# The shared expert of a mixture-of-experts layer, with weights and tokens exchanging places on TensorE

## The chip, the cores and the metric

The kernel runs on one core of one Trainium2 chip. The metric is the device time of one execution in microseconds (us). TensorE multiplies, VectorE (DVE), ScalarE (ACT) and GpSimd (POOL) work beside it, SyncE (SP) issues DMAs.

## The reference

2048 tokens of width 512 pass a pre-norm block: a linear attention with decay (16 heads), then a mixture of experts (8 experts of 352 hidden columns, the best two of each token) and one shared expert of 704 hidden columns, which all tokens pass.

```python
x = x + attn(layernorm(x))           # decayed running sums of k*v and k
x2 = layernorm(x)
g = silu(einsum('td,edh->teh', x2, w_gate)) * einsum('td,edh->teh', x2, w_up)
routed = einsum('teh,ehd,te->td', g, w_down, comb)
shared = silu(x2 @ sw_gate) * (x2 @ sw_up) @ sw_down
x = x + routed + shared
```

## The kernel before

Every factor is kept as two halves, an upper float16 and the lower rest, and every product is three products (upper x upper, upper x lower, lower x upper): `product`, line 591. The kernel writes out each engine's order by hand, with semaphores between engines; nothing plans it.

**Attention** takes four blocks of 512 tokens. Beside its last block the shared expert begins (lines 778 to 803), and its normalised rows go to a scratch in HBM, from where a transposing DMA brings tiles of 128 tokens back (`turn_tile`, line 900) into one of two buffers `xT[:, b]`.

**The shared expert** is 32 units: unit u is half u % 2 of the hidden columns (384, then 320) for the tile u // 2 of 128 tokens. A tile of x is the stationary operand, the weights stream past it. The result lies with tokens on the partitions, so the hidden values must be turned before the down product: `turn_chunk` (line 639) puts three 128x128 transposes between the next unit's gate products. A unit is, on TensorE (lines 805 to 831): gate(u+1) with turns of u, up(u+1), the beside work, down(u). Half 1 has a twin: the last 64 hidden columns stand in two copies, so that its last chunk needs two products and not three; 17 down products a tile. ScalarE (`gate_silu`, `upper_hidT`, lines 1274 to 1282) applies silu and copies the upper half; VectorE (`hidden`, `rest_hidT`, lines 1554 to 1578) multiplies and makes the lower half. Each pair of buffers passes a semaphore: `g_mm`, `u_mm`, `silu_s`, `hid_s`, `turned_h`, `hidTh_s`, `hidT_s`, `y_mm`, `y_s`.

**Beside the units** the 24 weight matrices of the eight experts are prepared, one piece per unit from unit 3 to 26: ScalarE squares it (`square`, line 1226, waits for the norm of the piece before), VectorE folds the squares (`fold`, 1588), TensorE sums columns (`column_norms`, 444, waits for the fold), VectorE takes the maximum (`column_max`, 1598), and one unit in three sets scales (`set_scales`, 1605). Units 8 to 30 split the pieces (`split_unit`, line 321; `upper` on ScalarE, 1245; `split` on VectorE, 1628), unit 19 two of them. ScalarE also issues the loads of experts 2 to 7 in units 5, 8, 11, 14, 17 and 20 (line 1371). VectorE chooses experts and builds the tables of jobs (`routing`, line 1968), with one-hots in the even units 10 to 24 (`one_hots`, 1914) that TensorE multiplies (`table_product`, 706). In iteration u each engine first does the unit's own steps, then this work in this order: VectorE one-hots, maximum, scales, split, fold, routing; ScalarE load, upper, square, y. On TensorE the norms of unit u come in iteration u + 1.

**The jobs** (line 833) are 36 groups of 128 rows of one expert, four of them pairs of 64 rows of two experts on two column tiles (`pair_product`, 601), with gathers and scatters by GpSimd (`gather`, `scatter`). A job is gate of the next, with the turns inside, up of the next, down of this one.

## Time and profile before

| | us |
|---|---|
| median of 3 runs | 656.45 (653.41 to 658.42) |
| profiled execution, its own time | 656.56 |
| its span in the trace | 654.8 |

| engine | busy us | share of the span |
|---|---|---|
| TensorE products (PE) | 625.2 | 95% |
| TensorE weight loads (PEld) | 416.1 | 64% |
| VectorE | 420.0 | 64% |
| ScalarE | 265.1 | 40% |
| GpSimd | 191.2 | 29% |

The stages, by TensorE's timeline: attention to 212.8 us, the seam in which attention ends and the shared expert begins to about 251, units of the shared expert to 422.0, jobs to about 645, last scatter and end to 654.8. The mean granted clock of TensorE was 0.988. Durations of TensorE's rows include its pipeline; what a product costs when they follow each other is the distance from start to start.

### The profile page before, as it was taken

What the parts mean: (1) busy time and instruction counts of PE and PEld (TensorE: products, weight loads), DVE (VectorE), ACT (ScalarE), POOL (GpSimd) and SP (SyncE); (2) the same over time, 40 slices, a digit from 0 to 9 for tenths busy, and PEclk for the clock granted to TensorE, in tenths of its full rate; (3) what the DMA queues carried; (4) which work ended last, traced back from release to release, by engine and by line L of the source; (5) the groups of instructions that cost most, each with busy time, mean ns of one, the idle gap of its engine ahead of it and who ended that gap; (6) DMA issues with size and microseconds to landing.
All of it is one profiled execution on the core that took longest, in us unless ns stands there. A gap on an engine that the chain in (4) does not pass through costs nothing.

```text
span 654.8 us, 11594 instructions
## 1 busy us (share of the span) xinstructions
PE 625.2 (95%) x3785; PEld 416.1 (64%) x3786; DVE 420.0 (64%) x831; ACT 265.1 (40%) x411; POOL 191.2 (29%) x250
## 2 busy tenths in 40 slices
PE   7999999999999999999999999999999999999992
PEld 7777777668677666556665556665666666555561
DVE  5998887997998954768867877633334334333331
ACT  4464653464444445466666766421111111111110
POOL 5220131231103226002111212134454354343422
PEclk8999999999999999999999999999999999998997
DMA  6851013513424796966664824469598679877743
GB/s 223 288 181 33 17 50 79 162 49 98 130 65 106 219 234 221 213 160 178 133 175 112 193 38 62 85 129 122 105 140 146 117 132 133 125 101 126 127 65 47
DMA packets 107136, 83.78 MB, mean 128 GB/s; under 512 B 77040, under 2 KB 83184, under 8 KB 107088
## 3 DMA queue, kind: packets, MB, share of 16 engines
q1 hardware_dynamic: 85744, 43.28, 29.4%
q0 software_dynamic: 12128, 26.88, 23.5%
q10 hardware_dynamic: 9216, 12.98, 6.2%
q8 instruction: 29, 0.48, 0.3%
q14 instruction: 19, 0.16, 0.1%
HBM read 43.80 MB, written 22.54 MB: 101 GB/s over the span
## 4 chain that ended last, share of the span: by engine, by line
PE 62%; DVE 5%; DMA 4%; issue 2%; SPq 1%; ACT 1%; ACTq 0%; POOL 0%; POOLq 0%; DVEq 0%
PE ps_y L597 16%; PE ps_g L597 15%; PE ps_u L597 14%; PE ring L441 8%; PE turn_h L647 3%; DMA out_dram<-y_job,job_tok 1%; PE ps_g L610 1%; DMA x_in<-x_job 1%; PE ps_u L610 1%; PE ps_y L610 1%; PE ps_y L664 1%; DMA out_dram<-x 1%; SPq L896 1%; DMA xg_odd<-xn_hl 1%; DMA x_job<-xn_scratch,job_tok 1%
## 5 line engine op out<-in xcount | busy, mean ns | idle before, releaser
L1282 ACT CAST hidT<-turn_h 128x384 f16<-128x384 f32 x68 | 32.5, 478 | 181.5 <-PE turn_h L647 181.5
L441 PE MATMUL ring<-xnT_h,wq_h 128*128 128x512 f32 x188 | 76.7, 408 | 2.7 <-DVE wq_l L1439 1.4
L597 PE MATMUL ps_g<-routed,x_in 128*128 x384 | 74.3, 316 | 2.4 <-DMA x_in<-x_job 2.4
L441 PE MATMUL ring<-xnT_h,wq_l 128*128 128x512 f32 x188 | 74.5, 396 | 0.0
L441 PE MATMUL ring<-xnT_l,wq_h 128*128 128x512 f32 x188 | 74.0, 394 | 0.0
L597 PE MATMUL ps_g<-shared,x_in 128*128 128x384 f16 (+1 forms) x384 | 72.3, 313 | 0.0
L1130 POOL DMA_INDIRECT out_dram<-y_job,job_tok x32 | 52.1, 1629 | 60.0 <-DVE y_job L1965 32.8
L597 PE MATMUL ps_y<-routed,hidT 128*128 x288 | 67.4, 379 | 1.3 <-DVE hidT L1562 1.3
L1577 DVE SCALAR_TENSOR_TENSOR hid<-ps_u,job_hid,silu 128x352 f32<-128x352 f32 x36 | 21.0, 584 | 66.9 <-PE ps_u L597 41.8
L597 PE MATMUL ps_u<-routed,x_in 128*128 x384 | 63.0, 314 | 0.0
L597 PE MATMUL ps_u<-shared,x_in 128*128 128x384 f16 (+1 forms) x384 | 62.5, 313 | 0.0
L1029 POOL TENSOR_SCALAR var_eps<-mean_var 128x1 f32<-128x1 f32 x32 | 11.5, 361 | 170.4 <-DVE mean_var L1542 92.7
L597 PE MATMUL ps_y<-shared,hidT 128*128 128x512 f16 x240 | 57.1, 379 | 3.9 <-DVE hidT L1562 2.3
L1965 DVE TENSOR_SCALAR y_job<-ps_y,job_y 128x512 f32<-128x512 f32 x36 | 27.0, 751 | 48.5 <-PE ps_y L597 43.1
L1107 POOL DMA_DIRECT2D out_dram<-y_job x16 | 14.2, 909 | 136.6 <-ACT y_job L1288 136.3
L647 PE MATMUL turn_h<-ident,hid 128*128 128x128 f32 x204 | 52.3, 274 | 0.0
L597 PEld LDWEIGHTS ps_g<-routed,x_in 128*128 128x128 f16 x384 | 37.6, 99 | 22.4 <-issue 5.0
L597 PEld LDWEIGHTS ps_u<-routed,x_in 128*128 128x128 f16 x384 | 37.8, 99 | 20.2
L597 PEld LDWEIGHTS ps_u<-shared,x_in 128*128 128x128 f16 x384 | 37.5, 98 | 19.8 <-DVE hid L1577 0.2
L597 PEld LDWEIGHTS ps_g<-shared,x_in 128*128 128x128 f16 x384 | 37.3, 98 | 20.0 <-issue 1.6
L1117 POOL DMA_INDIRECT x_job<-xn_scratch,job_tok x36 | 36.7, 1021 | 42.5 <-DMA x_in<-x_job 29.0
L597 PEld LDWEIGHTS ps_y<-routed,hidT 128*128 128x128 f16 x288 | 27.9, 98 | 31.7 <-issue 2.6
(301 smaller groups left out, 1191.1 us busy)
## 6 DMA issues: line engine op xcount, KB each, us to landing
x_res<-in_L_attn_x_dram SPq DMA_DIRECT2D x20, 256.0 KB, 3.2
routed<-in_L_ffn_w_gate_dram ACTq DMA_DIRECT2D x6, 704.0 KB, 4.8
routed<-in_L_ffn_w_up_dram ACTq DMA_DIRECT2D x6, 704.0 KB, 7.2
out_dram<-x SPq DMA_DIRECT2D x16, 256.0 KB, 3.5
xn_scratch<-xn_hl SPq DMA_DIRECT2D x16, 256.0 KB, 2.6
out_dram<-y_job POOLq DMA_DIRECT2D x16, 256.0 KB, 4.1
x_in<-in_L_attn_x_dram SPq DMA_DIRECT2D x12, 256.0 KB, 3.0
routed<-in_L_ffn_w_down_dram ACTq DMA_DIRECT2D x6, 512.0 KB, 8.2
```

The lines of the kernel that those rows point to most:

```text
L441: ins = pe.matmul(ps, a, b, start=(i == 0), stop=(i == len(steps) - 1))
L597: ins = pe.matmul(ps, a[i][:, k, :], w(j, k), start=(start and q == 0), stop=(stop and q == len(steps) - 1))
L610: ins = pe.matmul(ps[rows, :], a[i][:, k, rows], ws[h](j, k), start=(q == 0), stop=(q == len(steps) - 1), tile_position=(0, HALF * h))
L647: ins = pe.transpose(turn_h[:, c, :], hid[:, col:col + P], ident[:, :])
L664: ins = pe.matmul(ps_y[:, :], hidT[:, 0, FC - 1, :], w(j, FC - 1), start=False, stop=(stop and j == 1))
L1029: pool.tensor_scalar(ve, mv, LN_EPS, by, ALU.add, ALU.mult).then_inc(s[got], 1)
L1107: pool.dma_start(out[t * P:(t + 1) * P, :], y_job[:, t % 2, :], accum_op=ALU.add)\
L1117: pool.indirect_dma_start(x_job[:, b, :], None, xn2_d[:, :], bass.IndirectOffsetOnAxis(job_tok[:, r:r + 1], 0))\
L1130: pool.indirect_dma_start(out[:, :], bass.IndirectOffsetOnAxis(job_tok[:, r:r + 1], 0), y_job[:, b, :], None, bounds_check=T - 1, oob_is_e ...
L1282: act.copy(hidT[:, 0], turn_h[:, 0:FC, :]).then_inc(s["hidTh_s"], 1)
L1577: dve.scalar_tensor_tensor(out=hid[:, 0:n], in0=ps_u[:, 0:n], scalar=by, in1=silu[:, 0:n], op0=ALU.mult, op1=ALU.mult).then_inc(s["hid_s"], 1)
L1965: dve.tensor_scalar(y_job[:, b, :], ps_y[:, :], job_y[:, bass.ds(r, 1)], None, ALU.mult)\
```

## The change

The shared expert's weights become the stationary operand and two tiles of x (256 tokens) stream past them. The result lies with hidden columns on the partitions and needs no turn. 704 hidden columns are five whole steps of 128 and a rest of 64; the rest uses two column tiles for gate and up (one per tile of tokens) and two row tiles for down, so that a tile has 16.5 down products' time if both run at once. Six steps of a pair of tiles fill three iterations of u, the fourth holds the down products of both tiles, with the work beside them at chunk 3 of the second tile. gate and up alternate between two PSUM banks each (gate from the second pair of tiles on), the y results too. VectorE multiplies in place in PSUM. Silu, hidden values and y share SBUF in one buffer `work`, in which shared y has one slot. Both x tiles are fetched for the next pair when all up products of this pair are done. The first job's gate and up products now follow the last down product, and the jobs' turns stand in a row in front of the fourth gate product.

```diff
@@ constants
-    SHARED_F = (P * FC, HALVES * F - P * FC)
-    TWIN = P // 2
+    WHOLE = HALVES * F // P
+    REST = HALVES * F - P * WHOLE
+    STEPS = WHOLE + 1
+    SHARED_STEPS = STEPS * SBLOCKS
@@ banks
+        def gate_bank(h):
+            return ps_g if h < STEPS or h % STEPS % 2 == 0 else ps_gate
+        def up_bank(h):
+            return ps_u if h % STEPS % 2 == 0 else ps_u2
@@ product: the turns
-                    if inside is not None and 3 <= q < 3 + FC:
-                        inside(q - 3)
+                    if q == 3 and inside is not None:
+                        inside()
@@ TensorE, new
+            def shared_product(ps, h, kind):
+                ...
+                    if c < WHOLE:
+                        ins = pe.matmul(ps[:, 0:SBLK].rearrange("p (b q) -> p b q", b=2), w, xT[:, :, i * KC + k, :],
+                                        start=first, stop=last)
+                    else:
+                        for b in range(2):
+                            ins = pe.matmul(ps[REST * b:REST * (b + 1), 0:P], w, xT[:, b, i * KC + k, :],
+                                            start=first, stop=last, tile_position=(0, REST * b))
+            def shared_gate(h):
+                n, c = divmod(h, STEPS)
+                if c == 0:
+                    for b in range(2):
+                        pe.wait_ge(s[f"xin{b}"], 16 * (n + 1))
+                if 0 < h <= STEPS:
+                    pe.wait_ge(s["silu_s"], h)
+                elif h > STEPS:
+                    pe.wait_ge(s["silu_s"], h - 1)
+                if h == STEPS + 1:
+                    pe.wait_ge(s["rt_exp_in"], 1)
+                shared_product(gate_bank(h), h, 0).then_inc(s["g_mm"], 1)
+            def shared_up(h):
+                if h >= 2:
+                    pe.wait_ge(s["hidT_s"], h - 1)
+                shared_product(up_bank(h), h, 1).then_inc(s["u_mm"], 1)
+            def shared_down(n, between=None):
+                for b in range(2):
+                    ...
+                    for c in range(WHOLE):
+                        if b == 1 and c == FC and between is not None:
+                            between()
+                        pe.wait_ge(s["hidT_s"], STEPS * n + c + 1)
+                        for i, j in PARTS_OF:
+                            pe.matmul(y_bank(t)[:, :], hid_whole[:, c, i, b * P:(b + 1) * P], w(j, c), ...)
+                pe.wait_ge(s["hidT_s"], STEPS * (n + 1))
+                for i, j in PARTS_OF:
+                    for b in range(2):
+                        rows = slice(REST * b, REST * (b + 1))
+                        ins = pe.matmul(y_bank(b)[:, :], hid_rest[rows, i, :], w(j, WHOLE, rows), ...,
+                                        tile_position=(REST * b, 0))
@@ TensorE, the units
+            for u in range(2, HALVES * NT):
+                n, p = u // 4, u % 4
+                def beside():
+                    if u == 3:
+                        gate(last + 2)
+                        gate(last + 3)
+                    if norm_unit(u - 1) is not None:
+                        column_norms(norm_unit(u - 1))
+                    ...
+                if p == 3:
+                    shared_down(n, beside)
+                    continue
+                for h in (STEPS * n + 2 * p, STEPS * n + 2 * p + 1):
+                    shared_gate(h)
+                    shared_up(h)
+                    if u == 2:
+                        gate(last + h - 2 * p)
+                beside()
@@ SyncE
-                    sp.wait_ge(s["u_mm"], HALVES * (t - 1))
+                    sp.wait_ge(s["u_mm"], STEPS * (t // 2))
@@ ScalarE
+            def shared_silu(h):
+                act.wait_ge(s["g_mm"], h + 1)
+                if h:
+                    act.wait_ge(s["hid_s"], h)
+                act.activation(silu_sh[:, 0:n], gate_bank(h)[:, 0:n], ACT.Silu, ...)
+            def shared_upper(h):
+                act.wait_ge(s["hid_s"], h + 1)
+                act.copy(hidden_to(h, 0), up_bank(h)[:, 0:step_cols(h)]).then_inc(s["hidTh_s"], 1)
@@ ScalarE, the end of the seam: order
+            shared_upper(1)
+            rows_2(last + 1)
+            rows_2(last + 2)
+            shared_upper(2)
+            shared_silu(3)
+            rows_2(last + 3)
+            shared_upper(3)
@@ ScalarE, a unit: silu and upper of its two steps, then as before; y
+                if p == 3:
+                    move_y(2 * n)
+                if p == 0:
+                    move_y(2 * n - 1)
@@ VectorE
+            def shared_hidden(h):
+                dve.wait_ge(s["silu_s"], h + 1)
+                dve.wait_ge(s["u_mm"], h + 1)
+                dve.scalar_tensor_tensor(out=up, in0=up, scalar=hid_scale[:, E:E + 1], in1=silu_sh[:, 0:n], ...)
+            def shared_rest(h):
+                dve.wait_ge(s["hidTh_s"], h + 1)
+                dve.tensor_tensor(hidden_to(h, 1), up_bank(h)[:, 0:step_cols(h)], hidden_to(h, 0), ALU.subtract)
+            for u in range(2, HALVES * NT):
+                if p < 3:
+                    for h in (STEPS * n + 2 * p, STEPS * n + 2 * p + 1):
+                        shared_hidden(h)
+                        shared_rest(h)
@@ VectorE, first job
+                if first:
+                    dve.wait_ge(*tile_sem("yo", NT - 1))
```

## Rows read from the trace of the kernel before

**Rows 1.** Busy time by stretch, the rewritten stage; columns named in the first line.

```profile
core 0: us, PE busy (x) PEld busy (x) DVE busy (x) ACT busy (x) POOL busy (x), PEclk, DMA share, GB/s
...
251.20:422.00 170.80, 167.26 (x1063) 104.43 (x1062) 126.87 (x372) 108.52 (x137) 33.19 (x57) 1.00 0.61 140
```

**Rows 2.** Timeline of TensorE: start us, length us, engine, line, out<-in, count.

```profile
261.05 2.10 PE L597 MATMUL ps_y<-shared,hidT 128*128 128x512 f16 x9
262.99 0.65 PE L597 MATMUL ps_g<-shared,x_in 128*128 128x384 f16 x3
263.48 0.27 PE L647 MATMUL turn_h<-ident,hid 128*128 128x128 f32 x1
263.59 0.33 PE L597 MATMUL ps_g<-shared,x_in 128*128 128x384 f16 x1
```

**Rows 3.** Timeline of TensorE at the start, and the products of line 716 by duration.

```profile
13.94 1.50 PE L716 MATMUL ring<-ones_h 128*128 128x128 bf16 x24
...
L716 PE MATMUL ring<-ones_h x120: 219/219/314, 1.1 to 15.2; 128*128 128x128 bf16 x120
```

**Rows 4.** Timeline of TensorE in the first gate product of a pair job.

```profile
451.35 0.31 PE L610 MATMUL ps_g<-routed,x_in 128*64 x1
451.35 0.31 PE L610 MATMUL ps_g<-shared,x_in 128*64 128x352 f16 x1
451.50 0.31 PE L610 MATMUL ps_g<-routed,x_in 128*64 x1
...
451.75 0.55 PE L647 MATMUL turn_h<-ident,hid 128*128 128x128 f32 x3
452.22 0.34 PE L610 MATMUL ps_g<-routed,x_in 128*64 x1
```

**Rows 5.** Groups of VectorE, 262 to 420 us: busy us, mean ns, idle before.

```profile
L1633 DVE SCALAR_TENSOR_TENSOR routed<-routed,scale 128x1408 f16<-128x1408 f32 x16 | 26.9, 1678 | 5.0 <-ACT routed L1254 4.9
...
L1558 DVE TENSOR_TENSOR hidT<-turn_h,hidT 128x256 f16<-128x256 f32 x13 | 5.5, 421 | 0.9 <-ACT hidT L1282 0.7
```

**Rows 6.** The same view of ScalarE.

```profile
L1254 ACT ACTIVATE routed<-routed,scale 128x1408 f16<-128x1408 f32 x16 | 23.4, 1464 | 10.8 <-DVE routed L1633 6.8 <-issue 4.0
...
L1240 ACT ACTIVATE squares<-routed 128x1408 bf16<-128x1408 f32 x8 | 11.0, 1373 | 2.4 <-PE ps_norm L457 2.4
```

**Rows 7.** Timeline of VectorE in unit 10.

```profile
299.18 0.68 DVE L1921 TENSOR_TENSOR hot_p<-iota_p,slot_p 128x512 f16<-128x512 f32 x1
...
302.65 1.82 DVE L1633 SCALAR_TENSOR_TENSOR routed<-routed,scale 128x1536 f16<-128x1536 f32 x1
...
304.45 0.42 DVE L1558 TENSOR_TENSOR hidT<-turn_h,hidT 128x256 f16<-128x256 f32 x1
```

**Rows 8.** Timeline of VectorE in unit 5, the first slots.

```profile
269.82 0.28 DVE L1832 COPY score<-ps_rt 128x128 f32<-128x128 f32 x1
...
273.57 0.17 DVE L1855 TENSOR_TENSOR left_by<-left_by,whole_end 128x8 f32<-128x8 f32 x1
```

**Rows 9.** Timeline of ScalarE and its DMA queue (ACTq) in unit 8.

```profile
284.75 0.38 ACTq L423 DMA_DIRECT2D routed<-in_L_ffn_w_gate_dram  x1
...
287.25 1.47 ACT L1254 ACTIVATE routed<-routed,scale 128x1408 f16<-128x1408 f32 x1 [1.97 <-issue]
```

**Rows 10.** Timeline of ScalarE, the last attention tile.

```profile
242.57 0.62 ACT L1224 CAST xn_hl<-xn 128x512 f16<-128x512 f32 x1
```

**Rows 11.** DMA issues (KB, median us to landing), and the issue time of line 906.

```profile
out_dram<-y_job POOLq DMA_DIRECT2D x16, 256.0 KB, 4.1
...
xg_odd<-xn_hl SPq DMA_TRANSPOSE x8, 3.1
...
L906 SPq DMA_TRANSPOSE x_in<-xn_scratch x16: 1232/1281/1593, 184.3 to 397.2; - x16
```

**Rows 12.** TensorE behind a wait in the jobs, and the granted clock then.

```profile
590.34 0.62 PE L597 MATMUL ps_g<-routed,x_in 128*128 x3 [2.37 <-DMA x_in<-x_job]
...
592.00:594.00 2.00, 2.00 (x9) 1.01 (x8) 0.56 (x1) 0.33 (x2) 1.58 (x1) 0.50 0.51 143
```

More of the change, by code:

```diff
@@ L605, in pair_product @@
                     if q == 3 and inside is not None:
-                        for c in range(FC):
-                            inside(c)
+                        inside()
                     for h in range(2):
@@ new lines, in down_product @@
+            def down_product(u, t, w):
+                pe.wait_ge(s["hidT_s"], u + 1)
+                pe.wait_ge(s["y_s"], t)
+                product(ps_y[:, :], [hidT[:, h] for h in range(2)], w, FC, True, True).then_inc(s["y_mm"], 1)
+            halfword = lambda w, j, n, at, m: w[:, j * n + at:j * n + at + m]
+            PARTS_OF = ((0, 0), (0, 1), (1, 0))
+            def shared_product(ps, h, kind):
+                c = h % STEPS
+                steps = [(i, j, k) for k in chunks for i, j in PARTS_OF]
+                for q, (i, j, k) in enumerate(steps):
+                    w = halfword(shared_done[HALVES * kind + k // 2], j, GU, (k % 2) * HALVES * F + c * P,
+                                 P if c < WHOLE else REST)
+                    first, last = q == 0, q == len(steps) - 1
+                    if c < WHOLE:
[5 more added lines that the diff above has]
+                                            start=first, stop=last, tile_position=(0, REST * b))
+                return ins
@@ L992, in _ @@
                             turn_rows((n - 1) * TPB + j)
[L993 to L995 removed]
+            for t in range(2, NT):
                 turn_tile(t)
@@ L1577, in hidden @@
-                dve.scalar_tensor_tensor(out=hid[:, 0:n], in0=ps_u[:, 0:n], scalar=by, in1=silu[:, 0:n],
+                if r is not None:
+                    dve.wait_ge(s["turned_h"], r)
+                dve.scalar_tensor_tensor(out=hid[:, :], in0=ps_u[:, 0:F], scalar=by, in1=silu[:, :],
                                          op0=ALU.mult, op1=ALU.mult).then_inc(s["hid_s"], 1)
```

314 lines of the change are left out of this document (141 added, 173 removed).

## Prediction

> **What bounds the kernel now.** I read the span by stages first [rows 1]: from 251.2 us, where the third tile's first gate product starts, to 422.0 us, where the first job's does, lies the stage that the change rewrites. TensorE is busy for 167.3 of its 170.8 us at clock 1.00, so it is the bound and loses only 3.5 us to waits. VectorE is busy for 126.9 us there (74%) and ScalarE for 108.5 us (64%): they are hidden, but not idle, and how much room they keep is the question. Then I read TensorE's timeline for what one product costs. Nine products of 512 columns start at 261.05 and the next group at 262.99 [rows 2]: 215.6 ns each, start to start (the duration of one row holds the pipeline and isn't its cost). Products of 128 columns with 128x128 weights: 24 rows span 1.50 us, the last is 219 ns long, so (1.50 - 0.22)/23 = 55.6 ns [rows 3]. The line through both is n/2.4 + 2.3 ns: 109 ns for 256 columns, 162 for 384, 136 for 320. A turn between gate products adds 0.11 us (263.48 to 263.59) [rows 2].
>
> **What TensorE saves.** Before, for two tiles: gate and up are 48 products of 384 columns and 48 of 320, 14.3 us; 34 down products 7.33; 12 turns 1.32; together 23.0 us. After, for two tiles: five whole steps of 24 products of 256 columns, 120 x 109 ns = 13.1 us; the rest step; 30 down products, 6.47; the rest's down, six products in three couples of row tiles, between 3 x 216 ns = 0.65 (parallel) and 1.29 (one after another). The rest step has 24 couples of 128-column products on two column tiles. No row has this couple. Below, it costs one 128-column product, 55.6 ns [rows 3]; above, what a couple of 352 columns takes, 150 ns (451.35 to 451.50) [rows 4]. Those rows show both column tiles running at once, so I lean to the lower end but not onto it, since two weight loads must fit beside 53 ns of columns: 85 ns, 2.04 us. A change of tiling shows a gap, 0.10 us before the turns (451.50 + 0.15 to 451.75) and 0.14 behind them (0.47 less 3 x 0.11) [rows 4]: about 0.4 us for the four changes of a pair of tiles. With the rest's down at 0.65 (column tiles do run at once) this is 22.7 us: 0.3 us less than before, not the 1.3 us of the turns. The saved turns and the half product are nearly spent on short products.
>
> The Trainium skill, "TensorEngine Tiling (Array Packing)", Restrictions, says that column tiling disables Fast Weight Load, and "TensorE: Matmul & The Clock Gate", LDWEIGHTS, gives columns/1.2 ns for a plain load: 53 ns for 64 columns, 107 ns for a couple, so by these pages the rest step would be 24 x 0.107 = 2.6 us and the saving gone (an estimate). No row shows it: at 352 columns the load hides.
>
> **What takes the turns' place.** Step h now goes silu (ScalarE), product in place (VectorE), upper half (ScalarE), lower half (VectorE); up(h) waits for the lower half of h-2, gate(h) for silu(h-2). So TensorE may be two steps ahead, 5.2 us. Before, one unit's look-ahead was 6 us, and, more important, ScalarE was done with unit u+1's silu before its own other work, whereas now its last copy of a unit comes 1.2 us after TensorE's last product of that unit. The other work (call it the load of a unit) is unchanged: splitting an expert's piece costs ScalarE 1.4 us and then VectorE 1.6 [rows 5, 6], a square 1.3 [rows 6], the one-hots, a maximum and the scales 3.5 us of VectorE (299.18 to 302.65) and with the split and fold 5.3 us (to 304.45) [rows 7], the first slots 4.0 us [rows 8]. An expert's load holds ScalarE for 2.5 us (284.75 to 287.25) [rows 9]. And TensorE's column norms of unit u wait for the fold of u-1, which stands behind all this; they stand right behind the second step of a unit, or inside the down products at chunk 3 of the second tile.
>
> **One pair in full, units 16 to 19**, in us from its first gate product; small operations of 256 columns 0.35 to 0.4 [rows 5], handing over 0.1 to 0.3. Steps 0 and 1 end at 5.24, their lower halves at 6.85. Unit 16 on VectorE: one-hots to 8.3, maximum and scales to 10.35, split to 12.1, fold 12.2. TensorE ends step 3 and the last norms at 11.0 and waits to 12.2. Steps 2 and 3 get their halves by 14.95; step 4 and the rest end at 17.1. ScalarE issues the expert's load 14.5 to 17.0, upper half to 18.4; VectorE splits to 20.05, fold 20.15: TensorE waits 3.0. The down products run from 20.4, the norms in them come at 25.55, but unit 18 (halves 23.2, one-hots, scales, split, fold of gate weights) ends at 28.45: 2.9 more. The pair ends at 31.1, where TensorE's own work is 22.7, and 23.6 with the norms (352 columns), the tables (108) and the gaps beside them. The same working gives 29.2 for units 4 to 7 (the fold of unit 5 waits for a square behind a load, the first slots come behind it, and down chunk 4 waits for its half), 30.9 for 8 to 11, 27.2 for 12 to 15, 28.2 for 20 to 23, 25.6 for 24 to 27 and 23.7 for 28 to 31, where no load is left. Sum 195.9 against 170.8 before: **+25.1 us**.
>
> **The seams.** In front, silu(4) now stands behind the last tile's cast, which ends at 243.2 [rows 10]; then lower half and product of step 3, 245.3; rest step 247.3; gates and down products 7.9: pair 2 starts at 255.2, before it was 251.2: +4.0. At 422.0 the kernel of before still owed a down product and turns, 1.7 + 0.3: -2.0. At the end the two y copies share one buffer: copy, issue, landing 4.1 us [rows 11], twice, hold the first job's weighing on VectorE to about 11.5 us behind the last down product, 2 us after it could run; about +1 on TensorE. The next pair's two transposes are issued at the start of the down products: 1.3 each to issue and 3.1 from issue to landing [rows 11], 1.3 + 3.1 to 2.6 + 3.1 = 5.7, under 7.3 of down: nothing. The jobs' turns in a row cost nothing: in a row they are also 0.11 apart (0.47 with the gap) [rows 4], the gap there belongs to the change of tiling; the work hidden beside them is the same. If each of the 31 plain jobs showed the 0.14 gap it would be +4, if turning earlier helped, 0. Gates, gathers and scatters of the jobs stay as they are.
>
> **Sum.** The profiled execution took 656.6 us (span 654.8), 0.1 above the median of 656.45: 656.6 + 25.1 + 4.0 - 2.0 + 1.0 = **684.7 us**.
>
> **Rivals.** *Slower, as worked out*: 684.7. If half the waits are overrated, (195.9 - 165.2)/2 = 15 us less, 670; if row tiles run one after another and couples take 150 ns, up to 2.2 us a pair more where waits don't cover it, and each of the five waits over 2.2 us may halve the clock: after 2.37 us idle it is granted at 0.50, and 9 products start in 2.0 us where 2.0/0.149 = 13 would [rows 12]: 1 to 2 us each, 7 us in all, partly given back as VectorE gains that time. So 668 to 697.
> *Even*: VectorE and ScalarE keep up as they do now. 7 x 23.6 + 3.5 us of waits = 168.7, -2.1; with the seams +3.0: 657.5. For it: today's order hides 5.3 us of load, whose next lower half (304.45) came nearly in time [rows 7]. Against: in the pair above the room from the lower half to the moment that TensorE asks for the fold is 6.85 to 11.0, 4.1 us, in the first unit, and 14.95 to 17.1, 2.2 us, in the second.
> *Faster*: TensorE stays the bound and never waits (-2.1 - 3.5), both column tiles run wholly at once (24 x 0.03 x 8 = -5.8) and the front isn't late (-1.0): 644. It decides if the fold of a unit with split and scales ends less than 4 us (first unit) or 2 us (second) behind the lower half of its last step; below that every turn saved counts. VectorE's 74% speaks for it, the order of its work against.
> *Transposes late*: under an expert's load the second lands over 7.3 us after issue, on every pair 1 to 2 us, on top of the first case: about 700.
>
> **Numbers.** Slower as worked out 0.66, transposes late too 0.05, even 0.17, faster 0.12. The time is that of the first, 684. The range 652 to 697 takes in the even case and leaves out the faster one and the late transposes (0.17); the first case's own is 668 to 697. About 1% is what can be told from no change: faster 0.12, within 0.17, slower 0.71.
>
> **What would show it.** The stage up to the first job's gate should last about 199 us with TensorE idle for some 25 to 30 us, waiting for row sums or squares (the fold) and for the lower halves; the norms inside the down products should wait longest, in the units that split and set scales. In a stretch without experts (the last four units) a pair should take 23.7 us; over 24.5 means the rest step or the row tiles cost more than said. If the whole stage shows under 8 us of idle time, the step that fails is that the fold binds. If the plain jobs take longer than now, it is the turns in a row.

## The result, and the profile after

The changed kernel takes 688.22 us (median of 4 runs, 684.33 to 692.28) against 656.6 us for the kernel before on the same chip: ratio 1.0488, interval 1.0444 to 1.0532. It is 4.9% slower. The profiled execution took 686.96 us, with a span of 685.2. The forecast was 684, with 652 to 697.

First the stage that was rewritten, by pairs of tiles (busy time by stretch; the columns are those of [rows 1]). The first line is the whole stage, from the second pair's first gate product to the first job's, and answers to the line of [rows 1]:

```profile
256.70:451.80 195.10, 167.07 (x1496) 116.48 (x1496) 128.67 (x374) 107.02 (x162) 29.65 (x53) 0.97 0.49 121
256.70:287.40 30.70, 25.55 (x214) 17.34 (x214) 19.24 (x110) 12.49 (x22) 8.02 (x23) 0.94 0.63 170
287.40:319.00 31.60, 24.89 (x213) 16.39 (x211) 21.57 (x61) 17.05 (x25) 1.73 (x2) 0.95 0.62 171
319.00:345.50 26.50, 23.06 (x219) 16.68 (x217) 16.53 (x41) 16.38 (x24) 3.93 (x6) 1.00 0.49 127
345.50:376.60 31.10, 24.77 (x220) 16.95 (x218) 20.47 (x49) 16.74 (x25) 3.94 (x6) 0.96 0.44 110
376.60:404.00 27.40, 23.72 (x220) 16.64 (x218) 18.16 (x40) 18.34 (x27) 3.95 (x6) 0.99 0.50 123
404.00:429.10 25.10, 22.93 (x218) 16.57 (x217) 17.11 (x48) 16.09 (x25) 3.94 (x6) 1.00 0.28 48
429.10:451.80 22.70, 22.15 (x206) 15.91 (x204) 15.60 (x29) 9.93 (x17) 4.14 (x4) 1.00 0.37 71
```

TensorE is busy for 167.1 us, as before (167.3), and the stage is 24.3 us longer: TensorE stands still for 28.0 us where it stood for 3.5. VectorE and ScalarE have the same work as before (128.7 and 107.0 us busy; 126.9 and 108.5).

That TensorE's busy time is equal hides two things that cancel. The granted clock (third column from the end) is 0.94, 0.95, 0.96 and 0.99 in four of the pairs and was 1.00 before [rows 1]. The first of them alone lost (1 - 0.94) x 30.7 = 1.8 us, and the four 1.8 + 1.6 + 1.2 + 0.3 = 4.9 us. So the work itself is about 162 us, 5 less than before: the change did save TensorE work, and gave it back at the lower clock. Twelve down products behind a wait:

```profile
280.68 4.38 PE L737 MATMUL ps_y<-shared,work 128*128 128x512 f16 x12 [2.31 <-DVE work L1649]
```

They take 4.17 us to the next start (284.85), where twelve at the full clock take 2.59 (12 x 215.6 ns). The sum of the idle time by what ended it (waits in the window 250 to 450: engine, line, releaser, us in total, times, longest):

```profile
PE turn_h L483 <- DVE row_sum_h L1677: 15.3, 9, 3.4
PE turn_h L488 <- DVE squares L1679: 7.4, 4, 2.3
PE ps_y L737 <- DVE work L1649: 3.0, 3, 2.3
```

Lines 483 and 488 are the column norms, released by VectorE's fold: 22.7 us in 13 waits, 7.3 of them in three waits inside the down products (the longest, 3.40, among them) and 15.4 behind a unit's second step. Line 1649 is a lower half. The pair that the prediction worked out in full, units 16 to 19, starts at 345.55 (timeline of TensorE, its waits; VectorE and ScalarE around the second of them; the last bracket is the idle time and its releaser):

```profile
357.74 0.18 PE L483 MATMUL turn_h<-row_sum_h,ones_h 128*128 128x1 bf16 x1 [1.15 <-DVE row_sum_h L1677]
365.20 0.18 PE L483 MATMUL turn_h<-row_sum_h,ones_h 128*128 128x1 bf16 x1 [3.08 <-DVE row_sum_h L1677]
372.78 0.47 PE L488 MATMUL turn_h<-squares,ones_h 128*128 128x352 bf16 x2 [2.11 <-DVE squares L1679]
```

```profile
359.43 0.37 ACTq L454 DMA_DIRECT2D routed<-in_L_ffn_w_gate_dram  x1
...
360.40 1.39 ACTq L454 DMA_DIRECT2D routed<-in_L_ffn_w_down_dram  x2
361.89 1.47 ACT L1326 ACTIVATE routed<-routed,scale 128x1408 f16<-128x1408 f32 x1 [2.09 <-issue]
...
363.39 1.69 DVE L1717 SCALAR_TENSOR_TENSOR routed<-routed,scale 128x1408 f16<-128x1408 f32 x1 [3.07 <-ACT routed L1326]
364.99 0.15 DVE L1677 CAST row_sum_h<-row_sum 128x1 bf16<-128x1 f32 x1
```

This is the chain of one wait: ScalarE issues an expert's load for 2.4 us, then writes the upper half; VectorE idles 3.07 us for it, splits for 1.69, and only then comes to a cast of one column, for which TensorE has waited 3.08 us.

The seams (timeline of TensorE; the second fence is the first stretch of the jobs):

```profile
241.94 1.48 PE L691 MATMUL ps_g<-x_in,shared 128*128 128x256 f16 x12 [2.04 <-ACT work L1351]
...
246.07 0.86 PE L696 MATMUL ps_g<-x_in,shared 128*64 128x128 f16 x24 [1.15 <-ACT work L1351]
246.76 0.84 PE L696 MATMUL ps_u<-x_in,shared 128*64 128x128 f16 x24
...
256.70 1.47 PE L691 MATMUL ps_g<-x_in,shared 128*128 128x256 f16 x12 [1.16 <-issue]
```

```profile
451.06 0.82 PE L744 MATMUL ps_y<-shared,work 64*128 64x512 f16 x6
...
463.21 0.62 PE L628 MATMUL ps_g<-routed,x_in 128*128 x3 [1.80 <-DMA x_in<-x_job]
463.67 0.49 PE L671 MATMUL turn_h<-ident,work 128*128 128x128 f32 x3
464.00 0.31 PE L628 MATMUL ps_g<-routed,x_in 128*128 x1
```

The second pair starts 5.5 us later than before. The wait of 1.80 us at the third job is new: its tokens are gathered behind the shared expert's addition of tile 14, which now comes at the very end of the stage. From the first job to the end the spans leave 233.4 us, against 232.8 before, where 2.05 us of the stage's work were still owed.

### The profile page after: what moved, and what is told of

Its sections match the earlier page's. It is cut to its first block, busy times and chain, and to the rows that moved or that the text cites. A ratio compares the mean times of both kernels' runs of the same rounds, so it can differ in the third digit from the quotient of the medians.

```text
span 685.2 us, 12577 instructions
## 1 busy us (share of the span) xinstructions
PE 624.4 (91%) x4281; PEld 427.2 (62%) x4282; DVE 420.1 (61%) x831; ACT 267.0 (39%) x443; POOL 191.5 (28%) x250
## 3 DMA queue, kind: packets, MB, share of 16 engines
q1 hardware_dynamic: 85744, 43.28, 27.2%
## 4 chain that ended last, share of the span: by engine, by line
PE 36%; DMA 14%; issue 10%; DVE 9%; ACT 4%; POOL 3%; ACTq 1%; POOLq 0%; SPq 0%; DVEq 0%
DMA x_in<-x_job 10%; PE ring L472 8%; PE ps_g L628 5%; PE ps_u L628 5%; PE ps_y L628 5%; PE ps_y L737 3%; PE ps_u L691 2%; DMA x_job<-xn_scratch,job_tok 2%; DVE ps_u L1644 2%; DVE routed L1717 2%; PE ps_g L691 2%; ACTq L454 1%; PE turn_h L671 1%; PE ps_gate L691 1%; ACT routed L1326 1%
## 5 line engine op out<-in xcount | busy, mean ns | idle before, releaser
L628 PE MATMUL ps_y<-routed,work 128*128 x288 | 67.4, 379 | 1.3 <-DVE work L1654 1.3
L1661 DVE SCALAR_TENSOR_TENSOR work<-ps_u,job_hid,work 128x352 f32<-128x352 f32 x36 | 21.0, 584 | 72.3 <-PE ps_u L628 44.5
L1199 POOL DMA_INDIRECT out_dram<-work,job_tok x32 | 52.0, 1624 | 44.7 <-DVE work L2054 19.9
L737 PE MATMUL ps_y<-shared,work 128*128 128x512 f16 x240 | 57.8, 395 | 3.0 <-DVE work L1649 3.0
L691 PE MATMUL ps_u<-x_in,shared 128*128 128x256 f16 x480 | 59.0, 273 | 1.2 <-DVE work L1649 1.2
L2054 DVE TENSOR_SCALAR work<-ps_y,job_y 128x512 f32<-128x512 f32 x36 | 27.0, 751 | 50.4 <-PE ps_y L628 41.8
L1717 DVE SCALAR_TENSOR_TENSOR routed<-routed,scale 128x1408 f16<-128x1408 f32 (+1 forms) x24 | 41.5, 1728 | 20.3 <-ACT routed L1326 20.1
L691 PEld LDWEIGHTS ps_u<-x_in,shared 128*128 128x128 f16 x480 | 46.4, 98 | 8.3 <-DVE work L1649 2.1
L628 PEld LDWEIGHTS ps_y<-routed,work 128*128 128x128 f16 x288 | 27.8, 98 | 31.7 <-issue 2.6
L472 PEld LDWEIGHTS ring<-xnT_h,wq_h 128*128 128x128 f32 x188 | 35.3, 188 | 17.7 <-issue 6.5
```

The source lines that it names most:

```text
L472: ins = pe.matmul(ps, a, b, start=(i == 0), stop=(i == len(steps) - 1))
L628: ins = pe.matmul(ps, a[i][:, k, :], w(j, k), start=(start and q == 0), stop=(stop and q == len(steps) - 1))
L691: ins = pe.matmul(ps[:, 0:SBLK].rearrange("p (b q) -> p b q", b=2), w, xT[:, :, i * KC + k, :], start=first, stop=last)
L737: pe.matmul(y_bank(t)[:, :], hid_whole[:, c, i, b * P:(b + 1) * P], w(j, c), start=(c == 0 and i == 0 and j == 0), stop=False)
L1199: pool.indirect_dma_start(out[:, :], bass.IndirectOffsetOnAxis(job_tok[:, r:r + 1], 0), y_job[:, b, :], None, bounds_check=T - 1, oob_is_e ...
L1661: dve.scalar_tensor_tensor(out=hid[:, :], in0=ps_u[:, 0:F], scalar=by, in1=silu[:, :], op0=ALU.mult, op1=ALU.mult).then_inc(s["hid_s"], 1)
```

## The experiments

The kernel is slower for its waits; the question is what the waits hang on: the order of the work on ScalarE and VectorE, its amount, or a third thing. Each run is compared with the kernel before on the same chip. "Stage" is the time from the second pair's first gate product to the first job's, "idle" the sum of TensorE's listed waits from 250 to 450 us (to 430 without norms and in the last version, whose stages end there). That window takes in the wait just in front of the stage, 1.16 us in the changed kernel, which is why its 29.2 are not the 28.0 above. Stage and idle are of the one profiled execution, which lies up to 5 us from the median; stages of two executions can differ by about 3 us where nothing was changed (see the job turns).

| kernel | us | ratio to before, interval | stage | idle |
|---|---|---|---|---|
| before | 656.6 | | 170.8 | 3.2 |
| changed | 688.2 | 1.049, 1.044 to 1.053 | 195.1 | 29.2 |
| loads issued by SyncE | 678.7 | 1.033, 1.025 to 1.041 | 186.3 | 21.4 |
| split between the steps | 698.0 | 1.064, 1.055 to 1.073 | 207.1 | 34.1 |
| no norms | 669.7 | 1.021, 1.014 to 1.027 | 173.7 | 16.2 |
| job turns between products | 685.7 | 1.045, 1.038 to 1.053 | 191.8 | 25.9 |
| fold first | 685.9 | 1.047, 1.041 to 1.052 | 197.9 | 29.8 |
| front and gathers | 684.0 | 1.045, 1.039 to 1.050 | 195.2 | 28.7 |
| those orders together | 675.5 | 1.029, 1.025 to 1.034 | 189.2 | 21.9 |
| halves and squares apart | 679.1 | 1.036, 1.029 to 1.043 | 185.5 | 19.9 |
| all orders | 671.3 | 1.021, 1.015 to 1.027 | 185.5 | 17.5 |
| all orders, three mended | 665.9 | 1.012, 1.008 to 1.016 | 179.8 | 12.7 |

**The expert loads on another queue.** ScalarE's six issues of loads go to SyncE, behind the transposes.

```
-                        load_expert(act, e)          # ScalarE, units 5, 8, 11, ...
+                turn_tile(t)                         # SyncE
+                for e in loads.get(t // 2, ()):
+                    load_expert(sp, e)
```

> The changed kernel with the loads of experts 2 to 7 issued by SyncE behind the transposes of a pair of tiles instead of by ScalarE inside units 5, 8, 11, 14, 17 and 20. Theory (TensorE waits in the units because ScalarE and VectorE finish their other work too late): ScalarE gets 2.5 us back in six units, the waits behind those units (3.4, 3.1, 1.8 us and less) shrink, 676 to 683 us against 688. Rival A (TensorE's own short products and changes of tiling are what costs): no change, 688. Rival B (transfers are late): the loads now stand beside the transposes, 688 or slower.

Measured 678.66 us: 9.5 us less than the changed kernel, the intervals of the two ratios apart. The wait of 3.08 us above is 0.89 in this run. So the 2.4 us for which ScalarE issues a load stand in TensorE's way, as the sum said. Not all of it is gain: two loads now go out together, and a new wait of 3.69 us, for a silu, appears at 272.49, which comes back below.

**The split between the two steps.** The upper half and the split of an expert's piece go between the two steps of a unit, on both engines.

```
+                        if h % 2 == 0:               # ScalarE; VectorE the same with split(m)
+                            for m in split_pieces(u):
+                                upper(m)
```

> The changed kernel with only the order on ScalarE and VectorE changed: in the first three units of a pair of tiles the expert's piece is scaled (ScalarE) and split (VectorE) between the unit's two steps instead of behind the second; same instructions. Theory: 1.4 to 1.6 us leave the stretch between the second step's lower half and the fold on which TensorE waits, in 17 units of which about 11 make it wait: 674 to 682 us. Rival A: no change, 688.

Measured 698.0 us, 10 slower instead of 6 to 14 faster: this expectation was wrong. VectorE around one such split:

```profile
299.92 0.42 DVE L1652 TENSOR_TENSOR work<-ps_u,work 128x256 f16<-128x256 f32 x1 [0.44 <-ACT work L1356]
301.29 1.68 DVE L1720 SCALAR_TENSOR_TENSOR routed<-routed,scale 128x1408 f16<-128x1408 f32 x1 [0.94 <-ACT routed L1326]
302.89 0.48 DVE L1647 SCALAR_TENSOR_TENSOR ps_u<-ps_u,hid_scale,work 128x256 f32<-128x256 f32 x1
```

VectorE has just released the step's lower half and must now wait 0.94 us for ScalarE's upper half before it can split; only 3 us later (299.92 to 302.89) does it come to the next step's product. TensorE's waits for the fold are no shorter (23.0 us, against 22.7), and new ones, 4.3 us, stand at the rest step's up product. Read so, moving both members of a hand-over into the path of the steps puts the hand-over itself on the path.

**No norms.** The experts' squares, folds, norm products and maxima are left out; all experts take the shared expert's scales.

```
+        norm_unit = lambda u: None
...
-                dve.wait_ge(s["max_s"], SHARED_PIECES + 3 * (n - 1))
+                if x == E:
+                    dve.wait_ge(s["max_s"], SHARED_PIECES + 3 * (n - 1))
```

> The changed kernel without the column norms of the experts' weights: no squares, folds, norms and maxima (the experts take the shared expert's maximum for their scales); splits, scales, one-hots and loads stay. Theory: with the fold gone TensorE waits only for lower halves, a pair of tiles takes 22.5 to 25 us instead of 25 to 31.6, in all 656 to 665 us. Rival A: TensorE loses only its own norm products, under 4 us, 684 to 688.

Measured 669.73 us (664.94 to 671.30): right in direction, smaller than expected. The profile is of the fastest execution, 664.94. The fold's 22.7 us of waits are gone, but the stage kept 16.2 us of others, mostly on lower halves and silu (waits from 250 to 430 us):

```profile
PE ps_y L738 <- DVE work L1654: 5.3, 4, 2.4
PE ps_u L692 <- DVE work L1654: 4.9, 5, 1.6
PE ps_g L692 <- ACT work L1356: 3.8, 4, 1.3
```

Of 22.7 us taken away at the fold, about 10 come back at the next hand-overs (14.0 in these three kinds, against 3.0, 0.2 and 1.1 in the changed kernel). The fold binds, but it is only the first of several waits that would. The run takes work off both engines too, so by itself it doesn't tell order from amount.

**The job turns between the products again.**

```
-                    gate_product(u + 1, t + 1, 1 - b, gate_w, inside=lambda: turn_hidden(u))
+                    gate_product(u + 1, t + 1, 1 - b, gate_w, inside=lambda c: turn_one(u, c))
```

> The changed kernel with the turns of the plain jobs between the fourth, fifth and sixth gate product again, one each, as before the change. Theory (turns in a row cost 0.11 us each as they do in between): 688 within 0.5%, jobs of 5.85 us in both. Rival: each row of turns costs a gap of 0.14 us, then this is 4 us faster; or the earlier turn helps, then it is slower.

Measured 685.67 us (683.98 to 688.36), the changed kernel 688.22 (684.33 to 692.28): not told apart. The profiles say why. A plain job lasts 5.86 us, gate to gate, in both. In this run:

```profile
465.06 0.61 PE L628 MATMUL ps_g<-routed,x_in 128*128 x3
465.51 0.27 PE L678 MATMUL turn_h<-ident,work 128*128 128x128 f32 x1
465.62 0.31 PE L628 MATMUL ps_g<-routed,x_in 128*128 x1
```

A turn is 0.11 us from start to start here, and three in a row take 0.33 in the changed kernel (463.67 to 464.00): no gap. The 3.3 us by which the two spans' stages differ (191.8 and 195.1) lie in a part that this kernel does not touch; so much can two executions differ there.

**The fold first.** ScalarE squares before it writes upper halves; VectorE takes maximum, scales and fold before one-hots and split.

```
+                if norm_unit(u) is not None:
+                    square(norm_unit(u))             # ScalarE
                 for m in split_pieces(u):
                     upper(m)
```

> Kernel after, with two orders changed and nothing added: ScalarE squares a piece of an expert before it writes the upper halves of another piece, and VectorE folds the squares (and finds maximum and scales) before the one-hots and the split. Theory (the norm product stands in TensorE's order behind a fold that VectorE does last in its unit, behind one-hots of about 2.4 us and a split of 1.4 us that waits for its upper halves): the waits on the fold, 24.3 us in 13 waits in the changed kernel, fall to under 10, the waits on lower halves and silu stay within 5 us of what they were, and the time is 672 to 682. Rival (the two engines simply have too much to do in a unit; a wait taken away at the fold comes back at the next step's halves): 685 to 692, with the fold's waits turned into waits on work from the lower-half line. Rival from the split-between run: any reordering that makes VectorE wait for ScalarE earlier is slower: over 692.

Measured 685.93 us: the rival's. Waits from 250 to 450 us:

```profile
DVE row_sum_h L1677 <- ACT squares L1312: 19.2, 9, 3.7
...
PE ps_y L737 <- DVE work L1649: 7.9, 6, 2.5
...
PE turn_h L483 <- DVE row_sum_h L1677: 6.7, 5, 2.3
PE ps_u L691 <- DVE work L1649: 6.2, 8, 1.6
...
PE ps_rt L773 <- DVE hot_j L2009: 4.2, 4, 1.3
```

The fold's waits fall from 22.7 us (the expectation had put them at 24.3) to about 7, and lower halves and one-hots now take 18.3, where they took 3.2: VectorE now stands for 19.2 us before ScalarE's squares. The place of the fold alone is not the cause. That two blocks of ScalarE back to back (square and upper, 1.5 and 1.5 us) are longer than what TensorE can run ahead of a silu is a reading of these rows, not tested by itself.

**The front and the gathers.** None of the stage: hidden and rest of steps 1 to 3 before the last residuals and rows; the transposes of tiles 2 and 3 before those of rows 15; two gathers before the last shared additions.

```
-            rows_2(last + 2)
             shared_upper(2)
             shared_silu(3)
+            rows_2(last + 2)
```

> Kernel after, with three things changed, none in the stage between: at the front, hidden and rest of steps 1 to 3 go before residuals and rows of the last tiles on VectorE and ScalarE; the transposes of x tiles 2 and 3 go before the one of rows 15 on SyncE; and the third and fourth gather of the jobs go ahead of the shared expert's last additions on GpSimd. Theory (the front's waits of 0.99, 2.04, 1.15 and 1.16 us are a matter of order, and so is the 1.80 us before job 2): 3 to 5 us come off the front and 1.5 to 2 off the jobs, 681 to 684. Rival (the rows that are now later delay gate logits and the choice of experts, and everything hung on them): 686 to 690.

Measured 684.0 us, the upper end of what was expected. The ratio alone cannot tell this from the changed kernel; the trace can: the second pair starts at 255.06 without a wait, not 256.70, and the wait before the third job is gone. In front, one wait of 2.69 us has taken the place of 0.99, 2.04 and 1.15:

```profile
243.76 1.49 PE L696 MATMUL ps_g<-x_in,shared 128*64 128x128 f16 x24 [2.69 <-ACT work L1354]
```

**All four orders.** Loads, fold first, front and gathers, turns between.

> All of it together: the fold first, the front and the gathers as in the two runs above, the expert loads issued by SyncE, and the turns of the jobs between products again (which measured the same). If the parts are independent, 688 less 9.5 (loads) less 10 (fold) less 5 (front and gathers): 660 to 667. If waits that are taken away come back elsewhere: 670 to 678. It beats the kernel before (657) only if the stage between loses nearly all its 25 us of waits: not expected.

Measured 675.45 us, 8 above the range for independent parts. The range took 10 us for the fold first, which alone measured 2; with the parts as measured (9.5, 2.3 and 4.2 us) the sum is 672, and the run is 3 above it. Its largest wait by far (timelines of ScalarE, GpSimd and TensorE):

```profile
272.29 0.69 ACT L1390 ACTIVATE work<-ps_y,y_scale 128x512 f32<-128x512 f32 x1 [8.79 <-DMA out_dram<-work]
```

```profile
264.97 0.95 POOL L1194 DMA_DIRECT2D out_dram<-work  x1 [0.31 <-POOL zeros L1227]
```

```profile
273.40 2.74 PE L699 MATMUL ps_g<-x_in,shared 128*128 128x256 f16 x12 [5.05 <-ACT work L1369]
```

GpSimd issues the first shared addition at 264.97, behind its constants; it meets two experts' loads, now issued together; ScalarE waits for it to land before the next y copy, and behind that copy stands the silu for which TensorE waits 5.05 us. TensorE's next row then lasts 2.74 us, where the same row lasts 1.47 elsewhere. With one y buffer for both tiles, a slow store reaches TensorE in three steps. The run with the loads alone has the same wait at 3.69 us (ScalarE stands 7.43 us there): its 9.5 us are what is left after it.

**Halves and squares apart.** ScalarE's upper half goes between the steps, its square after the second; VectorE's one-hots go between the steps, its split stays last; and TensorE takes two of three row sums as they are (float32), without VectorE's cast.

```
+                        if h % 2 == 0:               # ScalarE only
+                            for m in split_pieces(u):
+                                upper(m)
...
+                if straight:
+                    pe.wait_ge(s["square_s"], m + 1)
```

> Kernel after, in the stage between alone: ScalarE writes the upper halves of an expert's piece between the unit's two steps and squares the other piece after the second (before: 2.65 us of both in one block after the second step); VectorE builds the one-hots between the steps and keeps the split at the end; and TensorE takes the row sums of two of three pieces as they are (float32), so that VectorE's cast, which stood behind its split, is gone from that chain. No work is added, 16 casts of a column are taken away. Theory (TensorE has one step of 2.6 us of cover, and any block of ScalarE or VectorE longer than that comes out as a wait): with blocks of at most 1.4 us on ScalarE and 2.4 on VectorE the 25 us of waits of the stage fall by 8 to 15 us: 673 to 680. Rival (the bound is the sum of the hand-overs between ScalarE and VectorE in a unit, whatever their order, as the fold-first run suggests): 683 to 690.

Measured 679.1 us (676.40 to 684.32): 9 less than the changed kernel, at the upper end of the theory's 673 to 680, and the stage's waits are 19.9 us. Set beside the split-between run it suggests that of the pair upper half and split, ScalarE's half may go early, because VectorE then finds it ready, and VectorE's half may not. But the run changes three things at once, and what each brings isn't separated. Apart from the loads (2.4 us, still on ScalarE here) no block of ScalarE's expert work is longer than about 1.6 us now. Of the work only 16 casts of one column are gone from VectorE; TensorE pays for them, since a row sum in float32 takes it 0.14 us where one in bfloat16 took 0.03.

**Halves and squares apart, loads, front and gathers, and job turns together**, with the first addition issued before GpSimd's constants. (The fold first and the split between the steps are not in it.)

> The same, and with it the parts that measured faster or the same: the loads issued by SyncE, the front's and the gathers' orders (the silu of the fifth step now ahead of the last rows on ScalarE), the turns of the jobs between products; and new, the first addition of a shared tile issued by GpSimd before its constants instead of after. In the run with all parts that addition went out at 265.0 us, landed behind two experts' loads, and ScalarE stood 8.8 us at its next tile; TensorE lost 5.05 us at 273.4 and then ran two products at half its clock (2.7 us more). Theory: those 7.7 us come back, and with the waits of the run above the time is 655 to 663; if only the addition's part holds, 666 to 669.

Measured 671.34 us, missed by 8. The addition's wait is gone, but the loads of experts 2 and 3 now stand in SyncE's queue before the transposes of the third pair (timeline of SyncE's queue, then of TensorE):

```profile
267.92 4.23 SPq L457 DMA_DIRECT2D routed<-in_L_ffn_w_down_dram  x2
272.24 8.26 SPq L997 DMA_TRANSPOSE x_in<-xn_scratch  x2
```

```profile
284.14 2.72 PE L711 MATMUL ps_g<-x_in,shared 128*128 128x256 f16 x12 [5.66 <-issue]
```

**Three orders mended**: load 3 behind the third pair's transposes, the fold before the scales, rows 15 before tiles 2 and 3.

> The kernel of the last run (671.3 us) with three orders mended that its trace names. One: SyncE issues the load of expert 3 after the transposes of tiles 4 and 5, not before (there they waited behind two experts' loads, TensorE stood 5.66 us at 284.14 and ran its next product at half its clock, 1.3 us more). Two: VectorE folds the squares of a gate's piece before it sets scales and splits (four waits on the fold, 0.72, 2.38, 3.07 and 0.32 us). Three: the transposes of x tiles 2 and 3 go behind those of rows 15 again (the last gate logits waited 1.58 us for rows 15). If each wait goes and none takes its place, 671.3 - 7.0 - 6.5 - 1.6 = 656 us, level with the kernel before (ratio 0.99 to 1.01). Rival (as in three runs so far, half of what is taken away comes back at another hand-over): 661 to 666.

Measured 665.91 us (10 runs, 661.10 to 670.87), between the sum (656) and the rival (661 to 666), at its upper end. Its stage lasts 179.8 us, with 12.7 us of waits in eight kinds by the list, the largest 4.5 us in four waits for lower halves. The front is level with before: the second pair starts at 251.86 (before: 251.2); from the first job on it takes 233.0 us (232.8). In the stage TensorE is busy for 167.3 us, as in the kernel before, and idle for 12.5 where it was idle for 3.5. So the difference to the kernel before is waits. It is the best version found, and it doesn't beat the kernel before: the interval of its ratio, 1.008 to 1.016, lies above 1.

**A control**: the same loads, addition and gathers in the kernel before.

> Control on the kernel before: its expert loads issued by SyncE between the transposes, its first shared addition ahead of GpSimd's constants and its gathers ahead of the last additions, as in the run beside it; nothing of the changed stage. If these orders matter only where TensorE waits on ScalarE and VectorE in the stage between, the kernel before, which waits about 3.5 us in its 200, has nothing to gain: 654 to 659, ratio 0.995 to 1.005. Rival (the loads on ScalarE cost the kernel before too): 648 to 652.

Measured 655.78 us, ratio 0.9975 (0.994 to 1.001): no difference that can be told. The 2.4 us of ScalarE per load cost the changed kernel 9.5 us and the kernel before at most the 4 us that the interval leaves. The waits belong to the changed order, not to the loads.

**Expert work out of the stage.** No norms, and all 24 uppers and splits moved behind the last unit, where TensorE waits for them in a block; its whole time (735 us) says nothing.

```
-            return [... for e in range(E) for i in range(3) if split_unit(e) + i == u]
+            return [... for e in range(E) for i in range(3) if u == HALVES * NT - 1]
```

> Kernel after without the experts' norms (all take the shared expert's scales, as in the run without norms) and with all 24 uppers and splits of the experts moved behind the last unit of the stage between, where TensorE then waits for them in one block of some 40 us. The whole time says nothing (about 690); what is read is the stage from the second pair's first product to the last down product. Theory (TensorE's own work in a pair is what its rows say, 22.2 us without norms, with the tables' products about 22.4, and all else in the 27.9 us of a mean pair is waiting on ScalarE's and VectorE's expert work): the seven pairs take 22.2 to 23.5 us each, 155 to 164 in all, against 195.1 in the changed kernel and 170.8 before, and the granted clock stays at 1.0. Rival (the hand-overs of the shared expert's own steps, silu, hidden, upper, rest, wait even when nothing else is in the way): 170 or more.

The stage takes 174.0 us (256.41 to 430.4), not the 155 to 164 expected. That is the rival's number, but for the most part not for the rival's reason. Its seven pairs are of two kinds: the first four take 27.9, 27.4, 27.2 and 24.8 us, the last three 22.4, 22.3 and 22.0. Two of the last:

```profile
386.10:408.40 22.30, 22.30 (x212) 16.37 (x210) 11.05 (x41) 5.83 (x14) 3.94 (x6) 1.00 0.33 54
363.80:386.10 22.30, 22.30 (x212) 16.42 (x212) 9.25 (x27) 5.32 (x13) 3.94 (x6) 1.00 0.61 152
```

These never wait. The theory is right for them: 22.3 us is TensorE's own work, with the tables' products. The first four wait for something else, the transposes of the next pair's x (SyncE's queue, then TensorE):

```profile
273.85 6.17 SPq L978 DMA_TRANSPOSE x_in<-xn_scratch  x2
```

```profile
284.33 2.53 PE L692 MATMUL ps_g<-x_in,shared 128*128 128x256 f16 x12 [2.21 <-DMA x_in<-xn_scratch]
```

Both tiles' x is free only after the last up product (273.6), so both transposes are issued then; beside an expert's load the two issues take 6.2 us, not 2.6 [rows 11], and they land 10.5 us after it, where the down products cover 8.5. Where no load is left, they are hidden. Of the 18 us that the stage lasts beyond 7 x 22.3, these four waits are 9.6, the lower clock behind three of them 5.0 (24 products take 4.28 us each time, and 2.62 at the full clock), and waits inside the first pair, for a silu, a lower half and a table, 2.5.

## Why the prediction was right

**The sum.** Forecast 684.7 for the profiled execution, measured 686.96. By its terms:

| term | forecast | measured |
|---|---|---|
| pair periods, seven | 29.2, 30.9, 27.2, 31.1, 28.2, 25.6, 23.7 | 30.7, 31.6, 26.5, 31.1, 27.3, 25.1, 22.7 |
| their sum less before's | +25.1 | +24.3 |
| front | +4.0 | +5.5 |
| owed at 422, and behind the stage | -2.0 and +1.0 | +0.6 together |

**The mechanism** held in its details: in units 16 to 19 the waits were forecast to end 12.2, 20.2 and 28.5 us after the pair's start, with 1.2, 3.0 and 2.9 us; they ended after 12.2, 19.7 and 27.2, with 1.15, 3.08 and 2.11. They are released by the fold, and the one of 3.08 stands behind a load, an upper half and a split. Of the signs that it gave, the idle time (28.0 of 25 to 30), the last pair and the plain jobs came out. Two did not: the stage of 199 us doesn't fit the forecast's own sum, 195.9 (195.1 measured), and the norms inside the down products have the longest single wait, but only 7.3 us of the fold's 22.7.

**What was luck.** The stage's sum is closer than its parts. Forecast were 165.2 us of TensorE's work and 30.7 of waits; measured are 162.2 of work at the full clock, 28.0 of waits and 4.9 lost at the lower clock. The sum put that last term at nothing and had it only in the range, as up to 7 us. So -3.0, -2.7 and +4.9 leave -0.8. The 31.1 us of units 16 to 19, forecast and measured, are a coincidence of the same kind: the last wait ended 1.2 us early, and the products behind it ran at the lower clock and took 3.46 us (373.19 to 376.65) where they take 2.15 (343.40 to 345.55).

**The saving.** TensorE's work was to shrink by 0.3 us in 23; it shrank by 1.0. Two tiles without experts took 23.06 us before, with one row sum in them, and take 22.0 now (the last pair of the run without expert work, 408.43 to 430.4). The last two tiles before start here, and the first job at 422.05:

```profile
398.99 0.65 PE L597 MATMUL ps_g<-shared,x_in 128*128 128x384 f16 x3
```

The mis-sized term is the rest couple, taken at 85 ns. The gate of the rest step starts at 246.07 and its up at 246.76: 12 couples in 0.69 us, 58 ns each, the lower bound of 55.6 [rows 3] to 2 ns. The rest step is 1.4 us and not 2.04. That is 0.65 of the 1.0 us by which the changed kernel's last pair, 22.7, stays under its forecast of 23.7; the rest is a wait of 0.55 where about 1 was allowed for. By the Trainium skill, column tiling disables Fast Weight Load ("TensorEngine Tiling (Array Packing)", Restrictions) and a load takes columns/1.2 ns ("TensorE: Matmul & The Clock Gate", LDWEIGHTS), 53 ns for 64 columns. The prediction's 107 for a couple also supposed that the two loads follow each other. The trace agrees with neither: one load is recorded at 110 ns,

```profile
L697 PEld LDWEIGHTS ps_gate<-x_in,shared x24: 106/110/111, 272.2 to 272.8; 128*64 128x64 f16 x24
```

but 24 of them start within 0.6 us, about 26 ns apart, so the loads overlap each other and the products. The row tiles' six products take 0.75 us (451.06 to 451.81), against 0.65 forecast for running at once and 1.29 one after another: at once, as forecast, with the change of tiling in it. A whole step's gate or up, 12 products of 256 columns, takes 1.31 us, 109 ns each, as forecast.

**The front** was 1.5 us short: ScalarE and VectorE were late as worked out, but it was not seen that the transposes of tiles 2 and 3 wait in SyncE's queue behind those of rows 15, which wait for a gate; the second pair lost 1.16 us to them.

**Behind the stage** 1.0 was forecast for the shared y buffer, 2.65 measured (0.6, and the 2.05 no longer owed); the step that was missed is a gather queued on GpSimd behind an addition, 1.80 us.

**The rivals.** *Even* (657.5) assumed that the two engines keep up, and *half the waits* (670), the lower bound, that they nearly do. They have the time: with the same work (126.3 and 106.1 us busy) and other orders the best version waits 12.5 us and not 28.0. *Faster* (644) rested on TensorE never waiting: its couples came true (58 ns, close to its 55), the rest didn't. *Transposes late* (5 in 100) did not happen, since the other waits gave the transposes time; it appears as soon as those are taken away, in the first four pairs of the run without expert work. *Job turns in a row* were neutral, as said.

**What stays open.** With 22.3 us a pair the stage would last 156 us, before norms. The best version has 179.8, of which 12.5 are waits. The remaining 11 are norms (with row sums in float32), gaps beside them and about 1.8 us lost at the lower clock (mean grant 0.99); they were not taken apart further. Whether a third accumulator for the up products would remove the rest of the waits wasn't tried, nor whether fetching each x tile earlier would.

## What to carry to other kernels

Count the hand-overs that a product's operand goes through and how far the array can run ahead of them, not only the products: here the change saved 0.7 to 1.0 us of TensorE's work in a pair of tiles (162.2 for 167.3 over seven pairs; 22.0 for 23.0 in a pair without norms) and bought 3.5 us of waits and 0.7 at the lower clock, because the room for ScalarE and VectorE shrank from a unit to a step. An engine that is 66% busy can still be the bound when its blocks are longer than that room; cut the blocks (halves and squares apart, with one-hots and casts: 9 us) or move them off the engine (loads: 9.5 us), and, as far as these runs go, move forward only the member of a hand-over whose input is ready. Read the clock beside the busy time: equal busy times were less work at a lower clock. And expect the next wait behind each one removed: three expectations that added the parts up came out 8 to 10 us short, one of them because a part put at 10 us measured 2.

## What the runs showed of the hardware

- Two 64-column tiles with 128 columns of x each: 58 ns a couple, as fast as one product of 128 columns on the whole array (55.6), though a weight load is recorded at 110 ns.
- A change from whole-array products to column tiles costs about 0.1 us (440.88 + 12 x 0.109 = 442.19, the next starts at 442.29).
- The granted clock after a wait. After 5.05 and 5.66 us of idle time the next 12 products of 256 columns take 2.5 us, not 1.31, and 2.3 after 2.21 (in the run without expert work); after 1.77 us nothing is lost. But in the changed kernel a wait of 2.31 us (at 280.68, above) is followed by the lower clock and one of 2.30 (at 396.00) is not: 24 products of 512 columns then start in 5.3 us; and after 3.08 us 24 products of 512 columns run at the full rate, while after the next wait, of 2.11, the clock falls (timeline of TensorE; then busy time by stretch, the clock third from the end):

```profile
365.33 5.34 PE L737 MATMUL ps_y<-shared,work 128*128 128x512 f16 x24
...
373.19 2.13 PE L737 MATMUL ps_y<-shared,work 128*128 128x512 f16 x6
```

```profile
365.30:369.30 4.00, 4.00 (x22) 1.88 (x22) 3.12 (x10) 3.07 (x5) 0.00 (x0) 1.00 1.09 266
369.30:372.80 3.50, 1.39 (x8) 0.43 (x7) 3.22 (x10) 0.88 (x2) 0.00 (x0) 1.00 0.00 0
372.80:376.60 3.80, 3.80 (x16) 1.16 (x16) 2.34 (x2) 1.85 (x2) 0.00 (x0) 0.64 0.02 4
```

  So the length of one wait doesn't decide it; what does, these runs leave open.
- A transposing DMA is issued in 1.3 us [rows 11], and in 3 to 4 us when experts' loads are under way: 6.17 and 8.26 us for two.
